# The normalised x turned by VectorE's 32x32 blocks and a way through HBM, in a fused cross-attention and expert-FFN kernel

## The reference, cut to what matters

```python
q = (layernorm(x) @ Wq);  k = ctx @ Wk;  v = ctx @ Wv        # 512 -> 4096
score = einsum('bqhd,bkhd->bhqk', q, k) / sqrt(128) + bias    # mask, softmax
x = x + (probs @ v) @ Wo
x = x + ffn(layernorm(x))     # base product, router, top-k, low-rank experts
```

## Time and profile before

| | us |
|---|---|
| median of 3 runs (786.52 to 787.85) | 786.58 |
| the profiled execution, its own time | 787.0 |
| its span in the trace | 785.2 |
| TensorE busy | 777.9 (99%) |
| VectorE busy | 524.9 (67%) |
| ScalarE busy | 399.8 (51%) |
| GpSimd busy | 184.5 (23%) |

### The profile page before, as it was taken

The page is one execution under the profiler, slowest core; times in us unless marked ns, Lnnn a source line. Parts: engine busy times, 40 slices in busy tenths (PEclk is TensorE's granted clock), DMA queues, the critical chain, the costliest instruction groups (busy, mean ns, idle before and its releaser), DMA issues.

```text
span 785.2 us, 16754 instructions
## 1 busy us (share of the span) xinstructions
PE 777.9 (99%) x6384; PEld 652.2 (83%) x6384; DVE 524.9 (67%) x951; ACT 399.8 (51%) x1138; POOL 184.5 (23%) x203
## 2 busy tenths in 40 slices
PE   9999999999999999999999999999999999999998
PEld 7888888888888888888888888888888888888886
DVE  5884626267677666677767776677667666758974
ACT  5662525246556455484664466545654565436520
POOL 0134041015325334232211222212221221010200
PEclk9999999999999999999999999999999999999999
DMA  6536674234554546584564575435553555231002
GB/s 228 200 122 215 217 242 146 109 134 162 176 173 158 167 163 188 175 262 125 176 203 113 161 176 186 134 97 175 162 152 110 144 162 162 91 99 56 2 8 100
DMA packets 108077, 118.38 MB, mean 151 GB/s; under 512 B 44239, under 2 KB 77007, under 8 KB 107998
## 3 DMA queue, kind: packets, MB, share of 16 engines
q1 hardware_dynamic: 107998, 117.31, 47.6%
HBM read 81.64 MB, written 35.65 MB: 149 GB/s over the span
## 4 chain that ended last, share of the span: by engine, by line
PE 95%; DVE 2%; ACT 1%; issue 1%; DMA 0%; ACTq 0%
PE pY L1395 43%; PE pP L1395 39%; PE pY L1556 4%; PE pO L1581 2%; PE pT_ L1581 1%; PE pO L1395 1%; PE pT_ L1566 1%; PE pS L1566 1%; ACT pr L761 1%; DVE st L982 1%; DVE y L1131 0%; PE pS L1581 0%; PE pO L1444 0%; PE pS L1444 0%; PE pY L1471 0%
## 5 line engine op out<-in xcount | busy, mean ns | idle before, releaser
L761 ACT ACTIVATE pr<-pr,mx 128x64 f32<-128x64 f32 x256 | 86.2, 344 | 28.7 <-DVE mx L1148 28.7
L1131 DVE TENSOR_TENSOR y<-y,pY 128x512 f32<-128x512 f32 x124 | 84.6, 682 | 22.6 <-PE pY L1395 22.4
L1395 PE MATMUL pY<-wo_hi,oT_hi 128*128 128x512 f32 x248 | 96.9, 391 | 0.5 <-DVE y L1131 0.4
L1395 PE MATMUL pY<-wo_lo,oT_hi 128*128 128x512 f32 x248 | 96.6, 390 | 0.0
L1395 PE MATMUL pY<-wo_hi,oT_lo 128*128 128x512 f32 x248 | 96.5, 389 | 0.0
L912 DVE TENSOR_TENSOR wk_lo<-wk_raw,wk_hi 128x256 fp32r<-128x256 f32 x96 | 49.8, 519 | 57.2 <-ACT wk_hi L653 56.2
L653 ACT CAST wk_hi<-twk 128x256 fp32r<-128x256 f32 x128 | 50.8, 409 | 65.2 <-PE pP L1395 53.4
L1395 PE MATMUL pP<-xo_hi,wk_hi 128*128 128x512 f32 x196 | 78.0, 398 | 0.6 <-DVE q L922 0.6
L1395 PE MATMUL pP<-xo_hi,wk_lo 128*128 128x512 f32 x196 | 76.5, 390 | 0.0
L1395 PE MATMUL pP<-xo_lo,wk_hi 128*128 128x512 f32 x196 | 76.4, 390 | 0.0
L586 POOL TENSOR_TENSOR bias<-bias,madd 128x512 f32<-128x512 f32 x32 | 41.8, 1320 | 145.7 <-DMA bias<-in_fside_Bx32xSxS 145.6
(11 more groups left out here) (282 smaller groups left out, 1899.5 us busy)
## 6 DMA issues: line engine op xcount, KB each, us to landing
v_hbm<-stage SPq DMA_DIRECT2D x64, 256.0 KB, 2.3
k_hbm<-stage SPq DMA_DIRECT2D x64, 256.0 KB, 3.4
k<-k_hbm SPq DMA_DIRECT2D x16, 1024.0 KB, 5.5
v<-v_hbm SPq DMA_DIRECT2D x16, 1024.0 KB, 7.3
wk_raw<-in_L_xattn_Wk SPq DMA_DIRECT2D x16, 512.0 KB, 4.3
wo_raw<-in_L_xattn_Wo SPq DMA_DIRECT2D x16, 512.0 KB, 3.6
bias<-in_fside_Bx32xSxS SPq DMA_DIRECT2D x128, 64.0 KB, 3.6
wk_raw<-in_L_xattn_Wq SPq DMA_DIRECT2D x16, 512.0 KB, 4.6
```

Of the source, the lines that this page charges most:

```text
L761: nc.scalar.activation(pr[s][:, b, :], pr[s][:, b, :], ACT.Exp, bias=mx[:, s, b:b + 1], accum_out=sm[:, s, b:b + 1]).then_inc(exp_made, 1)
L1131: nc.vector.tensor_tensor(y[:, t, :], y[:, t, :], src[:, :], ALU.add).then_inc(y_added, 1)
L1395: mm = nc.tensor.matmul(bank_, a, b, start=first and n == 0, stop=last and n == len(terms) - 1, skip_group_check=read_between)
```

## The change

TensorE no longer turns the x tiles. VectorE normalises two tiles into `xn` and turns each by 32x32 blocks (`nc.vector.transpose`, one instruction of 128x512) into `xb`. SyncE stores each of the two as 256 KB to `x_hbm`, and when a store has landed, loads it back in four pieces of 32 partitions (64 KB each, in runs of 512 B) into `first_x` and `low[1]`, so that the 32x32 blocks come to stand where a full transpose has them. That is ten DMAs for a pair, all in one place of SyncE's order, at the end of iterations 16, 19, 22 and 25. ScalarE and VectorE then read these two SBUF tiles in the place of the PSUM banks, and ScalarE's copy `rows_out` of the x tiles is gone. The moments move from the end of blocks 16, 19, 22, 25 to that of 15, 18, 21, 24, and `normalise` from 17, 20, 23, 26 to 16, 19, 22, 25. The pair is used in blocks 18, 21, 24 and 27, as before.

```diff
@@ SyncE
+            def turn_x(j):
+                for i in range(2):
+                    sp.wait_ge(xb_made, 2 * j + i + 1)
+                    sp.dma_start(x_hbm[2 * j + i], xb[:, i, :, :].rearrange("p a n -> p (a n)")).then_inc(put_x[i], 16)
+                if j >= 1:
+                    sp.wait_ge(sum_step, 4 * (4 + j))
+                    sp.wait_ge(a01_lo, 4 + j)
+                    sp.wait_ge(a6_lo, 4 + j)
+                for i, dst in enumerate((first_x, low[1])):
+                    sp.wait_ge(put_x[i], 16 * (j + 1))
+                    blocks = x_hbm[2 * j + i].rearrange("(t k) (a n) -> a k t n", t=4, a=4)
+                    for a in range(4):
+                        sp.dma_start(dst[32 * a:32 * a + 32, :, :], blocks[a]).then_inc(ld_xt[i], 16)
...
+                if 16 <= n < 28 and n % 3 == 1:
+                    turn_x((n - 16) // 3)
@@ GpSimd
-                if 16 <= n < 28 and n % 3 == 1:
-                    rstd_of((n - 16) // 3 * 2)
-                    rstd_of((n - 16) // 3 * 2 + 1)
+                if 15 <= n < 27 and n % 3 == 0:
+                    rstd_of((n - 15) // 3 * 2)
+                    rstd_of((n - 15) // 3 * 2 + 1)
@@ ScalarE
                 if j is not None:
                     first_high(j)
-                    rows_out(j)
                     last_high(j)
@@ VectorE, in sums_of_a(j)
+                        rows_ = second_of(j)
+                        for i in range(2):
+                            dve.wait_ge(ld_xt[i], 64 * (j - 3))
@@ VectorE, in normalise(n)
+                for i in range(2):
+                    m = 2 * n + i
+                    dve.wait_ge(xn_made, m + 1)
+                    if n >= 1:
+                        dve.wait_ge(put_x[i], 16 * n)
+                    nc.vector.transpose(xb[:, i, :, :].rearrange("p g (c q) -> p c g q", c=DC),
+                                        xn[:, i, :].rearrange("p (c g q) -> p c g q", c=DC, g=4)).then_inc(xb_made, 1)
@@ VectorE, the loop over n
+                if 15 <= n < 27 and n % 3 == 0:
+                    moments_of_x((n - 15) // 3)
                 if 16 <= n < 28 and n % 3 == 1:
-                    moments_of_x((n - 16) // 3)
-                if 17 <= n < 29 and n % 3 == 2:
-                    normalise((n - 17) // 3)
+                    normalise((n - 16) // 3)
@@ TensorE, the loop over n
                 times(n - 1, 4)
-                if prep_at(n) is not None:
-                    turn_pair(prep_at(n))
                 times(n, 6)
```

More of the change, by code:

```diff
@@ L93 @@
 DONE = {step: i + 1 for i, step in enumerate(ORDER)}
-FIRST_TURN = [0, 1, 4, 6, 8, 10, 12, 14]
-SECOND_TURN = [2, 3, 5, 7, 9, 11, 13, 15]
-NTURN = 16
+FIRST_TURN = [0, 1, 4, 6]
+SECOND_TURN = [2, 3, 5, 7]
+NTURN = 8
 SUM_ORDER = [1, 2, 3, 0, 4, 5, 6, 7]
@@ L127, in xattn_ffn @@
     k_hbm = nc.dram_tensor("k_hbm", (H, P, T), F32).ap()
+    x_hbm = nc.dram_tensor("x_hbm", (NT, P, D), F32).ap()
     with ExitStack() as stack:
@@ L204, in xattn_ffn @@
         sums_a = [at("sums_c", R2 + 2048, [P, 4, 2, P]), at("sums_x", R4 + 8192, [P, 4, 2, P])]
+        first_x = at("first_x", R4 + 14336, [P, 4, P])
         kept0 = [at("kept0_a", R2 + 6144, [P, 2, 2, P]), at("kept0_b", R2 + 8192, [P, DC, P])]
@@ L344, in raw_block, with first_of, second_of, like @@
             return raw[:, 2 * r:2 * r + 2, c * width:(c + 1) * width]
+        def first_of(j):
+            if j < 4:
+                return first_turn(j)[:, :].rearrange("p (c t) -> p c t", c=DC)
+            return first_x[:, :, :].rearrange("p t (c q) -> p c t q", c=DC)
+        def second_of(j):
+            if j < 4:
+                return second_turn(j)[:, :].rearrange("p (c t) -> p c t", c=DC)
+            return low[1][:, :, :].rearrange("p t (c q) -> p c t q", c=DC)
+        def like(j, a):
+            return a if j < 4 else a.rearrange("p c (t q) -> p c t q", t=4)
         def tw_of(w):
@@ L359, in tile_cols, with a01_of @@
             return slice(j % 4 * P, (j % 4 + 1) * P)
+        def a01_of(j, part):
+            return a_part(j, part)[:, 0:2, :, tile_cols(j)].rearrange("p k c t -> p (k c) t")
         def piece(n, i):
@@ L655, in first_high @@
             def first_high(j):
-                act.wait_ge(turned, FIRST_TURN[j] + 1)
-                nc.scalar.copy(a_part(j, 0)[:, 0:2, :, tile_cols(j)],
-                               first_turn(j)[:, :].rearrange("p (k c t) -> p k c t", k=2, c=2)).then_inc(a01_hi, 1)
+                if j < 4:
+                    act.wait_ge(turned, FIRST_TURN[j] + 1)
+                else:
+                    act.wait_ge(ld_xt[0], 64 * (j - 3))
+                nc.scalar.copy(like(j, a01_of(j, 0)), first_of(j)).then_inc(a01_hi, 1)
             def rows_out(j):
@@ L669, in last_high @@
             def last_high(j):
[L671 to L674, removed]
+                if j < 4:
+                    act.wait_ge(turned, SECOND_TURN[j] + 1)
+                else:
+                    act.wait_ge(ld_xt[1], 64 * (j - 3))
+                nc.scalar.copy(like(j, a_part(j, 0)[:, 6, :, tile_cols(j)]), second_of(j)[:, 2:4]).then_inc(a6_hi, 1)
             def sums_high(j):
@@ L945, in last_low @@
                 dve.wait_ge(a6_hi, j + 1)
-                lower(a_part(j, 1)[:, 6, :, cols], second_turn(j)[:, 2 * P:4 * P].rearrange("p (c t) -> p c t", c=2),
-                      a_part(j, 0)[:, 6, :, cols], a6_lo)
+                lower(like(j, a_part(j, 1)[:, 6, :, cols]), second_of(j)[:, 2:4],
+                      like(j, a_part(j, 0)[:, 6, :, cols]), a6_lo)
             def sums_of_a(j):
-                low_, s, k = low[j // 4], sums_a[j // 4], SUM_ORDER.index(j)
-                one = first_turn(j)[:, :].rearrange("p (k c t) -> p k c t", k=2, c=2)
+                s, k = sums_a[j // 4], SUM_ORDER.index(j)
+                s2, s3, s1, s4 = (like(j, s[:, n, :, :]) for n in range(4))
                 if j == 0:
-                    one, low_ = kept0
+                    a11, a12 = kept0[0][:, 0, :, :], kept0[0][:, 1, :, :]
+                    rows_ = kept0[1][:, :, :]
                     dve.wait_ge(kept0_made, 2)
                 else:
-                    dve.wait_ge(low_made, k + 1 if j < 4 else k)
+                    a11, a12 = first_of(j)[:, 0:2], first_of(j)[:, 2:4]
+                    if j < 4:
+                        rows_ = low[0][:, :, :]
+                        dve.wait_ge(low_made, k + 1)
+                    else:
+                        rows_ = second_of(j)
+                        for i in range(2):
+                            dve.wait_ge(ld_xt[i], 64 * (j - 3))
                 if k >= 1:
                     dve.wait_ge(as_lo, k)
-                nc.vector.tensor_tensor(s[:, 2, :, :], low_[:, 0:2, :], low_[:, 2:4, :], ALU.add).then_inc(sum_step, 1)
+                nc.vector.tensor_tensor(s1, rows_[:, 0:2], rows_[:, 2:4], ALU.add).then_inc(sum_step, 1)
                 if j >= 3:
@@ L964, in sums_of_a @@
                 dve.wait_ge(sum_step, 4 * k + 1)
[L965 to L968, removed]
+                nc.vector.tensor_tensor(s2, s1, a11, ALU.subtract).then_inc(sum_step, 1)
+                nc.vector.tensor_tensor(s3, a11, rows_[:, 0:2], ALU.subtract).then_inc(sum_step, 1)
                 dve.wait_ge(sum_step, 4 * k + 2)
-                nc.vector.tensor_tensor(s[:, 3, :, :], one[:, 1, :, :], s[:, 0, :, :], ALU.subtract
-                                        ).then_inc(sum_step, 1)
+                nc.vector.tensor_tensor(s4, a12, s2, ALU.subtract).then_inc(sum_step, 1)
                 if j >= 1:
@@ L1014, in normalise @@
                 for m, t in ((2 * n, n), (2 * n + 1, n + 4)):
-                    b = m % NX
+                    b, i = m % NX, m % 2
                     dve.wait_ge(rstd_made, m + 1)
-                    if m >= NX:
-                        dve.wait_ge(turned, 8 + m - NX + 1)
-                    nc.vector.tensor_scalar(xn[:, b, :], y[:, t, :], mv[:, b, 0:1], rstd[:, b:b + 1],
+                    if m >= 2:
+                        dve.wait_ge(xb_made, m - 1)
+                    nc.vector.tensor_scalar(xn[:, i, :], y[:, t, :], mv[:, b, 0:1], rstd[:, b:b + 1],
                                             ALU.subtract, ALU.mult).then_inc(xn_made, 1)
+                for i in range(2):
[5 more added lines that the diff above has]
+                                        xn[:, i, :].rearrange("p (c g q) -> p c g q", c=DC, g=4)).then_inc(xb_made, 1)
             def first_t3():
```

20 lines of the change are left out of this document (6 added, 14 removed).

## The result

The changed kernel takes 800.13 us in the median of 4 runs (798.29 to 802.96), the one before 787.06 (786.52 to 787.85): 1.0168 times as long, 95% interval 1.0134 to 1.0203. The sign is as forecast, the size is not: 13.1 us slower where 3.2 had been counted, and outside the range of 783.0 to 794.5. The profiled execution took 798.29 us with a span of 796.5, 11.3 us more than that of before.

A forecast was written before the change was run, and what follows sets the result against it. TensorE, busy for 99% of the span, was taken as the bound. Waits of 6.5 us less 3.56 of removed turning gave +2.9, with 0.3 for margins +3.2: 789.8 us against the median, 790.2 profiled; range 783.0 to 794.5.

The forecast's parts named there:

- 6.5 of waits before p7: TensorE before p7 of blocks 18, 21, 24, 27: waits of 1.62 us for each of four pairs, from late weights.
- less 3.56: TensorE's removed turning of the x tiles: 0.89 us a pair, 3.56 us for four pairs, all on the path.
- 0.3 for margins: Allowance of 0.3 us for margins that are gone in one or two of the pairs, making +2.9 into +3.2.
- each step of the queue: SyncE's added chain: transposed tile, store, eight loads, next store, weights issued at 183.51, 6.8 us late, then C11 and p7.
- C11(17) was hidden as counted: VectorE's C11 of block 17 would release p7(17) at 178.36, due at 179.22: hidden by 0.86 us.
- the moments in the same block: VectorE, 1.6 us before C11 of block 19: p7(19) hidden by 0.7 us, 0 to 0.5 us kept for each of three pairs.
- The pace of the loads: SyncE's issues of the eight loads: 0.60 us each taken, between bounds of 0.36 and 0.65.
- step 2: SyncE's eight loads of 64 KB: 4.80 us at 0.60 each, the last out at 183.15.
- steps 1 and 2: SyncE: first store issued at 176.25, landed at 178.35; then eight loads in 4.80 us, last out at 183.15.
- step 4: Weights land 4.3 us after issue, 187.85 with the wake-up; higher(7, 0) on ScalarE stalls for 3.9 us.
- a rival, at 1 us: Weights land in 5.3 instead of 4.3: another 1 us a pair, 793.5; chance 0.18 together with slow transpose.
- what is late next: After p7(18): C22(18) on VectorE, some 0.5 us ahead of p4(18), then C11(19) with no margin left.

The follow-up runs named there:

- experiment 1: Changed kernel with the eight x-tile loads one iteration later in SyncE's order, behind the K weights' load: 785.69 us, 0.9981 of before.
- experiment 2: Changed kernel without the way through HBM: block transposes made, neither stored nor loaded, the two tiles filled once from x: 785.52 us, 0.9977 of before.
- experiment 3: Kernel before, TensorE still turning, with ten DMAs of the same shapes added in the same places of SyncE's queue: 791.08 us, 1.0051 of before.
- experiment 8: Changed kernel with the eight loads behind the weights' load and VectorE's first_low of the x tiles behind the four sums: 785.00 us, 0.9974 of before.
- experiment 6: Changed kernel with VectorE's first_low of the x tiles moved behind the four sums: 797.35 us, 1.0135 of before.
- experiment 5: Kernel before with TensorE's turning of the x tiles taken out and nothing in its place, old PSUM contents read: 786.52 us, 0.9995 of before.
- experiment 7: Changed kernel with the eight loads of the first pair only put behind the next weights load: 796.62 us, 1.0122 of before.
- experiment 4: Kernel before with only the moments and the normalising one block earlier, TensorE turning as before: 786.69 us, 0.9994 of before.
- experiment 10: Changed kernel with only the first tile's four loads of each pair, the second tile filled once with rows of x: 789.54 us, 1.0048 of before.
- experiment 9: Experiment 8 with eight 32x32 transposes on TensorE in each place where the turning stood: 785.40 us, 0.9985 of before.

## Why the prediction was wrong in size

**The sum.** Forecast: 6.5 of waits before p7, less 3.56, and 0.3 for margins, +3.2. Measured in the profiles, to the first scores: 7.9 before p7, 3.4 on v_s, 1.4 at the lower clock, 0.5 of first steps, less 3.56; behind them 1.8. That is 11.4 where the spans differ by 11.3. The median of the changed kernel lies another 1.8 above its profiled run.

**What held.** The bound, the worth of the turning on TensorE (3.56 counted; 3.35 and 3.33 seen from block 14 to the first scores in experiments 1 and 2), and each step of the queue, in its order: transposes 0.63 apart for 0.62; first tile turned at 176.06 for 176.20; first store landed at 178.55 for 178.35; last load out at 183.12 for 183.15; weights at 183.69 for 183.51. That the change would make the kernel slower through the DMAs' place in SyncE's queue is shown by experiments 1, 2 and 3: the same bytes and the same passes of VectorE, with the loads behind the weights, lose nothing. C11(17) was hidden as counted, and the moments in the same block cost nothing.

**Right by luck.** The pace of the loads. A full issue takes 0.43 and the next starts 0.47 after it, not 0.60; eight are 3.8 us, not 4.8. In the first pair one issue of 1.33 made up for it, and step 2's end came out to 0.03 us; in the others the last load is out 5.7 us after the first store's issue, where steps 1 and 2 had 6.9. The nearest row was that of a tile of x, 0.43, not of the partial bias loads.

**The step that failed first: step 4, "it lands 4.3 later".** In the changed kernel the weights landed 5.61, 5.38, 4.39 and 4.66 us after their issue, behind eight loads and with three stores at once. The mean is 5.0, so the term was 0.7 too small. The forecast had this as a rival, at 1 us. It makes up for the pace: the four waits before p7 are 7.9 us by starts where the sum had 6.5. It differs by execution: fifteen such loads behind eight others, in four profiles, landed in 4.3 to 5.6, six of them in over 5.2; of thirteen in the kernel before none took over 4.9. In experiments 1 and 8, where the weights go ahead of the eight loads, they land as late, 4.2 to 5.7, so the order among the loads is not what delays them.

**The term that was missing, and the larger error: "what is late next".** I had named C22 and C11(19), and priced them at 0.3. What came was the copy v_s. On ScalarE it stands behind the high part of the four sums, which waits for VectorE's sums, which stand behind a C11 that is already late and behind `first_low`, which I had at 0.1 to 0.2 more than from PSUM and which took 0.54 more (1.22 for 0.68), because of GpSimd. TensorE's p3 waits for v_s: 3.4 us. The long pass makes most of it, since in experiment 6 two waits of 0.36 are left when it stands elsewhere; lateness makes the rest, since experiment 3 has 0.12 to 0.41 with the short pass. And v_s had only some 0.4 us of margin before, less than the turning that was taken out: in experiment 5 that alone makes p3 wait.

**A row misread.** I took the 0.58 us of the earlier trace rows for the price of two inputs in SBUF. But the low part of the earlier trace rows that I held against it has two inputs in SBUF as well, and took 0.41. The sum of 0.58 starts at 189.12 while a sum of GpSimd runs (188.68, 0.74 long). The same sums take 0.41 in the changed kernel with both inputs in SBUF. Two inputs in SBUF cost nothing by themselves; they cost the end of GpSimd's sum where one is under way.

**Not thought of: the clock.** A stretch at 1.2 GHz cost 1.4 us in the profile. The mean clocks of the four runs are 0.997 for 798.29, 0.998 for 799.06, 0.996 for 801.21 and 0.993 for 802.96. A mean of 0.993 is half the clock for 1.4% of 803 us, 11 us, of which 5.6 are lost at most, since a low clock costs nothing in a wait; at 0.997 it is 2.4, at 0.996 3.2. That can be 3.2 of the 4.7 us between the profiled run and the slowest, but only 0.8 of the 2.9 for 801.21, and nothing for 799.06. The rest isn't known. What makes the clock fall is left open: experiments 6 and 7 contradict the length of the wait alone.

**And behind the K blocks.** A gain on TensorE is not kept whole. Of 3.3 to 3.6 us won between block 14 and the first scores in experiments 1, 2 and 8, medians keep 1.2 to 1.6; the removal alone (2.4 won in its profile) keeps nothing in the median. The holes that end on "issue" come to 0.8 to 1.2 us in the profiles of the three kernels with the turning (before, 3 and 4), to 1.5 to 3.3 in eight without it (after, 1, 2, 5 to 8, 10) and to 0.9 in experiment 9, whose stream has its old length again. That the removal moves these holes is shown by experiment 9. That it makes them dearer is not: experiment 5 has 1.5. The largest, 1.4 to 1.7 us and some 400 us behind the first scores, is in five of the eight (after, 1, 6, 7, 10) and missing in three (2, 5, 8), and nothing here tells why.

## What to carry to other kernels

Before a chain of DMAs goes into a queue that also carries loads with a deadline, take the deadline (here 2.9 us of margin for the weights) and compare it with issue count times the issue time in that queue, plus one landing for every wait on a store; put the chain behind the load, not ahead of it. When a wait is forecast, follow it through every engine that is in order behind it and look for passes that will slide beside another engine's use of SBUF; the second wait was almost half of the first. Removing work from the busiest engine also takes margin from everything that it waits for later. On an engine at 99%, the time of removed work is the most that can be won: compare it with holes further on before building an elaborate way around it.

## What the runs showed of the hardware

- A 32x32 block transpose of 128x512 float32 on VectorE takes 0.68 us (0.658 to 0.699, 8 of them), and the second of a pair starts 0.63 behind the first; the statistics pass over as many takes 0.68 too. The Trainium skill (VectorE: DVE Perf Modes, The three transpose paths) has 311 ns for 128x128 bf16. Four of these, an estimate of 1.24 us, are not what 512 columns of float32 take.
- One issue of a DMA on SyncE takes 0.43 us for 64 KB in 32 partitions and for a tile of 256 KB alike; now and then one takes 1.1 to 1.65 (seven of the profiles have one of 1.09 to 1.65 among these loads, where the median is 0.43). The 50 ns of the Trainium skill (DMA: Bandwidth & Descriptors, Anatomy of one DMA) stand in a table on DMAs that GpSimd issues. The prediction took them for SyncE's queue; one issue holds this queue for some eight times as long.
- A VectorE pass with two SBUF inputs was held for the whole of a GpSimd sum that had begun before (0.84 us for 0.41 in experiment 6, 1.22 for 0.68 in the changed kernel); one with a PSUM input was not (0.68 in experiment 3).
- The granted clock fell to 0.50 at the end of a wait of 3.35 us and stayed there for 2.8 us behind it; it fell also behind waits of 1.81 and 2.26, but not behind those of 2.38 and 2.93.
- Holes in runs of small matmuls that no recorded event ends moved from 175, 252 and 329 to 330 to 97 to 99, 277 to 279 and 354 to 357 us behind the first scores when 32 matmuls were taken out ahead of them, and back when 32 small ones were put in.
